# Routed attention: GpSimd's inverse roots move ahead of the low part of the keys

## The chip, the cores and the metric

The kernel runs on one core of a Trainium2 chip. The metric is the time of one execution on the device in microseconds (us). Five engines work side by side, each on its own list of instructions in a fixed order: TensorE (PE in the rows; PEld is its weight load), VectorE (DVE), ScalarE (ACT), GpSimd (POOL) and SyncE (SP, which here only issues transfers). They meet at semaphores. An engine that waits for one holds up everything behind it in its own list.

## The reference, cut to what matters

The program is a stack of four layers, each an attention and a feed-forward part, on x of 8 batches x 256 tokens x 256 features. The change lies in the third layer's second part, an attention whose output is scaled by a gate (a "routed" attention). For each of the 8 batches:

```
q, k, v = heads(x @ Wq.T + bq), heads(x @ Wk.T + bk), heads(x @ Wv.T + bv)   # 16 heads of 16
q_norm  = q / norm(q, axis=-1)                                               # one root per token and head
q_scaled = (q_norm + query_embedding) * softplus(temperature)
attn = softmax(q_scaled @ k.T / sqrt(16));  h = attn @ v
out = h * masked_gates.sum(-1) ;  x = x + out @ Wp.T + bp
```

The root that the change is about is `1 / norm(q)`: 128 partitions x 2 tiles of tokens x 16 heads, so 128x32 numbers for each batch.

## The kernel before, in words

`attention16` works on two layers in one pipeline: a plain attention (batches 0 to 7) and the routed one (batches 8 to 15, called the first to eighth routed batch here). `head_steps` builds one list of steps. In step s, eight slots n = 0 to 7 are filled: the products of scores for head pair n of batch s - 3 (`score`), the products for the row maxima of head pair n of batch s - 2 (`max`), and behind them the slot's extras from the table `ROUTED_EXTRAS` (routed batches) or `HEAD_EXTRAS` (plain ones). An extra ("k", 0) is the keys of batch s, ("y", 5) the output product of batch s - 5. Every compute engine walks the same list from top to bottom and takes the items that concern it. So the table sets the order on every engine at once.

For the queries of a routed batch the items are, in this order:
- `q`: TensorE makes the queries, tokens on the partitions; VectorE adds the bias into `qtm` (L922).
- `square`: ScalarE squares them into `qsq` (L732).
- `sums`: VectorE sums the squares over each head into `qn` (L930).
- `roots`: GpSimd makes the inverse roots: a first guess (`root_guess`, L1449), three times the four instructions of `root` (L1467 to L1473), one product with the temperature (L685). That is 14 instructions on 128x32 numbers, one behind another.
- `scale`: VectorE multiplies `qtm` by the roots (L936). A TensorTensor with both inputs in SBUF.
- `qT`: TensorE turns `qtm` over (L337), ScalarE copies the result twice (`qf`, whole, and `qs`, rounded), GpSimd subtracts the two for the low part of the queries (L653, tile `a_sb_qs`).

For the keys, item `k`: TensorE (L788), ScalarE's two copies `kf` and `ks` (L717), and GpSimd's low part (L653, tile `a_sb_ks`, helper `rest`). When that is done, SP may send the keys out to device memory (`k_out`, L591), from where later issues bring them back in another order (`k_in`, L603 and L604). GpSimd has three more items: `norm` (the next batch's normalised rows, L220 to L230, roots, L209), `v` (adds the output bias to x, L692), and `qT` above.

SP has a list of its own, `MOVES`, that is the same for every step. For a routed step it reads: row of maxima out and in for the second half of the heads, keys in, queries out, queries in, then `neg0_out` (L609: the negated maxima of the first eight heads to device memory), `k_out`, `neg0_in` (L615: back into one row of `QP`). TensorE waits for `neg0_in` before item `score0` of the next step (L861), and before `max0` it waits until VectorE has read the product of the `max` item before (L838 and L1018; one PSUM tile `MX` serves all of them).

Slot 7 of a routed step holds `score7`, `max7`, `qT`, `factor`. In the first four routed steps the output product `y` of a plain batch (L795) follows there, before the next step's `score0`; in the last four `score0` follows at once.

Of the kernel before, what the change touches and what calls it, by code (L numbers as in the profile page):

```python
# [362 lines left out]
def at_least(eng, sem, count):  # L363
    if count > 0:
# [4 lines left out]
               2: [("weigh0", 3), ("T0", 4), ("T1", 4)], 3: [("k", 0)], 4: [("neg0", 2), ("weigh1", 3), ("aT", 4)],  # L369
               5: [("v", 0), ("out0", 3), ("norm", -1)], 6: [("weigh2", 3)], 7: [("y", 4)]}  # L370
ROUTED_EXTRAS = {0: [("neg1", 3), ("xT", 0), ("weigh3", 4), ("y", 5)], 1: [("q", 0), ("out1", 4), ("norm", -1)],
# [3 lines left out]
MOVES = [("ctx", -1, (False,)), ("neg1_out", 3, (False, True)), ("q_in", 1, (False,)), ("neg1_in", 3, (False, True)),  # L375
         ("k_in", 1, (False, True)), ("q_out", 1, (True,)), ("q_in", 1, (True,)), ("q_out", 0, (False,)),
# [2753 lines left out]
```

How the kernel before makes its waits and increments, by code:

```python
        @block.vector  # L166
        def _(dve):
            dve.wait_ge(loaded, 32)
            for t in range(NT):
                dve.bn_stats(g.stats[:, t, :], g.x[:, t, :])
# [2 lines left out]
def norm_factors(dve, g, sqrt_in, sqrt_out):  # L173
# [2 lines left out]
    dve.tensor_tensor(g.mean[:], st[:, :, 1], st[:, :, 4], ALU.add)  # L176
    dve.tensor_tensor(tmp[:, 0, :], st[:, :, 1], st[:, :, 4], ALU.subtract)
    dve.tensor_tensor(tmp[:, 1, :], st[:, :, 2], st[:, :, 5], ALU.add)
    dve.drain()
    dve.tensor_scalar(g.mean[:], g.mean[:], 0.5, None, ALU.mult)
    dve.tensor_tensor(tmp[:, 0, :], tmp[:, 0, :], tmp[:, 0, :], ALU.mult)
    dve.tensor_scalar(tmp[:, 1, :], tmp[:, 1, :], 1.0 / D, EPS, ALU.mult, ALU.add)
    dve.drain()
    dve.scalar_tensor_tensor(out=tmp[:, 1, :], in0=tmp[:, 0, :], scalar=0.25, in1=tmp[:, 1, :],
                             op0=ALU.mult, op1=ALU.add).then_inc(sqrt_in, 1)
    dve.wait_ge(sqrt_out, 1)
    dve.reciprocal(g.rstd[:], tmp[:, 2, :])
    dve.drain()
# [10 lines left out]
def norm_sqrt(act, g, sqrt_in, sqrt_out):  # L200
    act.wait_ge(sqrt_in, 1)
    act.activation(g.tmp[:, 2, :], g.tmp[:, 1, :], ACT.Sqrt).then_inc(sqrt_out, 1)
# [67 lines left out]
    def add(self, dve, g, b):  # L270
        dve.wait_ge(self.landed[b], 16 * TT * self.n)
        xb = g.x[:, b * TT:(b + 1) * TT, :]
        if self.layer == 1:
            dve.tensor_tensor(xb, xb, self.rows[:, b, 0], ALU.add)
# [88 lines left out]
def at_least(eng, sem, count):  # L363
    if count > 0:
        eng.wait_ge(sem, count)
# [164 lines left out]
        def scored(eng, b):  # L530
            eng.wait_ge(ex_full[1], 8 * (b + 1))
```

## Time and profile before

| | |
|---|---|
| median of 3 runs | 1793.23 us (1793.08 to 1796.47) |
| the profiled execution | 1801.62 us, of it 1799.9 in the span |
| PE busy | 1456.1 us (81%) |
| DVE | 979.6 us (54%) |
| ACT | 703.6 us (39%) |
| POOL | 551.8 us (31%) |
| mean granted TensorE clock | 0.893 of full speed |

The profile is of one execution; the span is the part that the trace covers. A busy share is over the whole span and does not tell which wait counts; the stretch of the routed batches is read by itself. The tile names in rows have no layer number: `a_sb_qn` there is the tile `a2_sb_qn` of this pipeline. The routed batches' roots run from 1043.9 to 1216.4 us.

### The profile page before, as it was taken

What the parts mean: (1) busy time and instruction counts of PE and PEld (TensorE: products, weight loads), DVE (VectorE), ACT (ScalarE), POOL (GpSimd) and SP (SyncE); (2) the same over time, 40 slices, a digit from 0 to 9 for tenths busy, and PEclk for the clock granted to TensorE, in tenths of its full rate; (3) what the DMA queues carried; (4) which work ended last, traced back from release to release, by engine and by line L of the source; (5) the groups of instructions that cost most, each with busy time, mean ns of one, the idle gap of its engine ahead of it and who ended that gap; (6) DMA issues with size and microseconds to landing.
All of it is one profiled execution on the core that took longest, in us unless ns stands there. A gap on an engine that the chain in (4) does not pass through costs nothing. (4 is left out here: it accounts for less than half of the span.)

```text
span 1799.9 us, 33526 instructions
## 1 busy us (share of the span) xinstructions
PE 1456.1 (81%) x12090; PEld 1131.0 (63%) x12090; DVE 979.6 (54%) x2007; ACT 703.6 (39%) x1554; POOL 551.8 (31%) x905
## 2 busy tenths in 40 slices
PE   3898676692889844997479999898769999999876
PEld 2565455581666524997346666665468888888765
DVE  2676463353765652221666676776346666666652
ACT  1465443230456520211246666664443333333111
POOL 2110016105655403000511455540035454444210
PEclk9799988796899966999689999997779999999976
DMA  5332093344865228994755555552030000000001
GB/s 142 87 73 50 2 365 130 115 133 150 189 147 134 60 87 310 339 351 168 212 121 131 122 105 119 120 117 51 2 114 7 8 8 7 8 1 2 2 7 47
DMA packets 89772, 195.49 MB, mean 109 GB/s; under 512 B 14000, under 2 KB 62513, under 8 KB 81041
## 3 DMA queue, kind: packets, MB, share of 16 engines
q1 hardware_dynamic: 76688, 172.97, 34.1%
q0 software_dynamic: 4608, 12.59, 2.2%
q10 hardware_dynamic: 8320, 7.87, 1.3%
q8 instruction: 96, 1.57, 0.4%
q14 instruction: 60, 0.48, 0.1%
HBM read 136.37 MB, written 57.02 MB: 107 GB/s over the span
## 5 line engine op out<-in xcount | busy, mean ns | idle before, releaser
L1018 DVE TENSOR_REDUCE a_sb_mx<-a_mx 128x4 f32<-128x1024 f32 x192 | 234.8, 1223 | 119.6 <-PE a_mx L838 117.1
L759 ACT ACTIVATE a_sb_probs<-a_ex 128x512 f32<-128x512 f32 x368 | 200.3, 599 | 150.8 <-PE a_ex L861 150.5
L1434 DVE RECIPROCAL a_sb_rden<-a_ot 128x256 f32<-128x256 f32 x64 | 111.5, 1742 | 60.8 <-PE a_ot L1297 60.8
L266 POOL DMA_INDIRECT a_sb_landing<-f_y_slots,g_pos x48 | 47.3, 985 | 264.0 <-POOLq L143 250.5
L838 PE MATMUL a_mx<-a_sb_KP,a_sb_QP 48*128 48x256 f32 x768 | 91.1, 315 | 36.4 <-DVE a_sb_mx L1018 24.3
L874 PE MATMUL a_ot<-a_sb_probs,a_sb_v 128*32 128x256 f32 x1536 | 112.9, 415 | 7.5 <-ACT a_sb_probs L759 7.5
L861 PE MATMUL a_ex<-a_sb_QP,a_sb_KP 49*128 49x256 f32 x736 | 95.7, 338 | 26.1 <-ACT a_sb_probs L759 20.3
L861 PEld LDWEIGHTS a_ex<-a_sb_QP,a_sb_KP 49*128 49x128 f32 x736 | 59.3, 194 | 78.2 <-issue 54.0
L1219 ACT ACTIVATE a_sb_whole<-a_gp 128x512 f32<-128x512 f32 x64 | 38.2, 598 | 170.4 <-PE a_gp L1241 170.4
L838 PEld LDWEIGHTS a_mx<-a_sb_KP,a_sb_QP 48*128 48x128 f32 x768 | 64.3, 201 | 48.8 <-DVE a_sb_mx L1018 25.9
L1173 POOL TENSOR_TENSOR a_sb_q_lo<-a_sb_whole,a_sb_q_hi 128x512 fp32r<-128x512 f32 x32 | 42.1, 1316 | 126.9 <-ACT a_sb_q_hi L1220 126.0
L1419 DVE TENSOR_REDUCE a_sb_mx<-a_sc 128x2 f32<-128x256 f32 (+1 forms) x128 | 62.0, 548 | 31.1 <-PE a_sc L1266 30.9
L1619 POOL TENSOR_SCALAR_AFFINE_SELECT a_sb_sim<-a_sb_sim 128x256 f32<-128x256 f32 x128 | 55.6, 464 | 63.9 <-ACT a_sb_sim L1674 63.9
L1231 ACT ACTIVATE a_sb_probs<-a_sc 128x512 f32<-128x512 f32 x64 | 38.2, 598 | 94.3 <-PE a_sc L1281 62.3
L2812 PEld LDWEIGHTS f_hb<-f_sb_xsT,f_sb_wb 128*128 128x128 f32 x640 | 74.3, 195 | 0.8 <-issue 0.3
L2812 PE MATMUL f_hb<-f_sb_xsT,f_sb_wb 128*128 128x128 f32 x640 | 74.5, 278 | 0.0
L653 POOL TENSOR_TENSOR a_sb_qs<-a_sb_qf,a_sb_qs 128x512 fp32r<-128x512 f32 x24 | 30.7, 1279 | 137.9 <-ACT a_sb_qs L717 101.7
L874 PEld LDWEIGHTS a_ot<-a_sb_probs,a_sb_v 128*32 128x32 f32 x1536 | 42.5, 114 | 45.3 <-issue 14.1
L2825 PE MATMUL f_yb<-f_sb_wb,f_sb_hT 128*128 128x256 f32 x320 | 70.7, 379 | 0.0
L1181 POOL TENSOR_SCALAR_AFFINE_SELECT a_sb_probs<-a_sb_probs 128x256 f32<-128x256 f32 x128 | 48.8, 404 | 60.8 <-ACT a_sb_probs L1232 60.7
L2758 ACT ACTIVATE f_sb_hT<-f_hb,f_sb_wb 128x128 f32<-128x128 f32 x80 | 22.8, 368 | 112.1 <-PE f_hb L2812 112.1
L1303 PE MATMUL a_gp<-a_sb_wo,a_sb_oT 128*128 128x256 f32 x256 | 61.6, 396 | 5.5 <-issue 5.5
(445 smaller groups left out, 3655.5 us busy)
## 6 DMA issues: line engine op xcount, KB each, us to landing
f_sb_wb<-f_w SPq DMA_DIRECT2D x20, 2052.0 KB, 10.1
a_q_moved<-a_sb_qs SPq DMA_DIRECT2D x24, 512.0 KB, 5.9
a_sb_QP<-a_q_moved SPq DMA_DIRECT2D x48, 256.0 KB, 4.4
a_k_moved<-a_sb_ks SPq DMA_DIRECT2D x16, 512.0 KB, 5.1
a_sb_KP<-a_k_moved SPq DMA_DIRECT2D x32, 256.0 KB, 6.0
a_sb_kvT<-ctxT SPq DMA_DIRECT2D x24, 256.0 KB, 3.0
a_sb_QP<-a_q_moved SPq DMA_DIRECT2D x48, 128.0 KB, 5.1
f_x_slots<-f_sb_zero SPq DMA_DIRECT2D x1, 6144.0 KB, 20.6
```

The lines of the kernel that those rows point to most:

```text
L759: act.activation(probs[:, group % 3, 2 * (u % 2) + par], ex_of(par, b, u)[:], ACT.Exp, scale=scale)\
L838: op = pe.matmul(MX[:, par, t, :], QP[at:at + R, b % 3, u, t * P:(t + 1) * P], KP[at:at + R, b % KB, u % KM, :], start=True, stop=True)
L861: op = pe.matmul(ex_of(par, b, u)[:, t, :], KP[at:at + R + 1, b % KB, u % KM, t * P:(t + 1) * P], QP[at:at + R + 1, b % 3, u, :], start=Tr ...
L874: op = pe.matmul(OT[c // 2][32 * j:32 * j + 32, c % 2, :], v4[:, b % 4, t, (4 * c + j) % VH, :], probs[:, (4 * b + c) % 3, j, t, :], start ...
L1018: dve.tensor_reduce(pair, MX[:], AX.X, ALU.max, negate=True).then_inc(mx_read, 1)
L1181: op = pool.affine_select(later, later, [[0, 2], [1, P]], ALU.is_ge, 0.0, base=0, channel_multiplier=-1)
L1303: op = pe.matmul(GP[gp.slot(("y", b))][:, t, :], oT[:, c, t * P:(t + 1) * P], wo[:, c, :], start=(c == 0), stop=(c == C - 1))
L1419: op = dve.tensor_reduce(mx[:, t, 2 * i:2 * i + 2], SC[pair][:, :, t, 0:(t + 1) * P], AX.X, ALU.max, negate=True)
L1434: dve.reciprocal(rden[:, n], OT[n][:, 1, :])
L1619: op = pool.affine_select(later, later, [[0, 2], [1, P]], ALU.is_ge, 0.0, base=0, channel_multiplier=-1)
L2812: op = pe.matmul(HB[j % 2][c // (FC // 2)][:, c % (FC // 2), :], w1(j, k, c), xsT[:, j, k, :], start=(k == 0), stop=(k == KD - 1))
L2825: op = pe.matmul(YB[j % 2][:, 0], hT[:, j, c, :], w2(j, c), start=(c == 0), stop=(c == FC - 1))
```

## The change

In `ROUTED_EXTRAS`, `sums` and `roots` come first in slot 3 and `k` behind them. Before, `k` and `sums` stood in slot 3 and `roots` in slot 4.

```diff
@@ -369,8 +369,8 @@
- 2: [("square", 0), ("weigh0", 3), ("T0", 4), ("T1", 4)], 3: [("k", 0), ("sums", 0)],
- 4: [("neg0", 2), ("weigh1", 3), ("aT", 4), ("roots", 0)], 5: [("gate", 4), ("out0", 3)],
+ 2: [("square", 0), ("weigh0", 3), ("T0", 4), ("T1", 4)], 3: [("sums", 0), ("roots", 0), ("k", 0)],
+ 4: [("neg0", 2), ("weigh1", 3), ("aT", 4)], 5: [("gate", 4), ("out0", 3)],
```

On GpSimd, the place between two batches' low parts of the queries in the last four routed steps. Before (`a_sb_ks` is the low part of the keys, `a_sb_qn` the roots, `g_x_all` the bias on x):

```order
L653 TENSOR_TENSOR a_sb_ks<-a_sb_kf,a_sb_ks 128x512
L1449 TENSOR_SCALAR a_sb_qn<-a_sb_qn 128x32
L1467 TENSOR_TENSOR a_sb_qn<-a_sb_qn 128x32
...
L1473 TENSOR_TENSOR a_sb_qn<-a_sb_qn 128x32
L685 TENSOR_TENSOR a_sb_qn<-a_sb_qn,a_sb_spq 128x32
L692 TENSOR_TENSOR g_x_all<-g_x_all,a_sb_bo 128x512
L653 TENSOR_TENSOR a_sb_qs<-a_sb_qf,a_sb_qs 128x512
```

The same place on GpSimd after the change:

```order
L1449 TENSOR_SCALAR a_sb_qn<-a_sb_qn 128x32
L1467 TENSOR_TENSOR a_sb_qn<-a_sb_qn 128x32
...
L1473 TENSOR_TENSOR a_sb_qn<-a_sb_qn 128x32
L685 TENSOR_TENSOR a_sb_qn<-a_sb_qn,a_sb_spq 128x32
L653 TENSOR_TENSOR a_sb_ks<-a_sb_kf,a_sb_ks 128x512
L692 TENSOR_TENSOR g_x_all<-g_x_all,a_sb_bo 128x512
L653 TENSOR_TENSOR a_sb_qs<-a_sb_qf,a_sb_qs 128x512
```

The low part of the keys has moved from ahead of the 14 root instructions to behind them, and stands directly ahead of the bias on x. This is so in all eight routed batches; nothing else moves on GpSimd, and the lists of PE, DVE, ACT and SP are the same in both kernels.

On SP, the transfers around the keys' way out in a routed step, the same before and after (`a_neg_moved` are the negated maxima in device memory, `a_k_moved` the keys):

```order
L609 DMA a_neg_moved<-a_sb_negT 8x256
L591 DMA a_k_moved<-a_sb_ks 128x2x512
L615 DMA a_sb_QP<-a_neg_moved 1x1024 x2
L609 DMA a_neg_moved<-a_sb_negT 8x256
L615 DMA a_sb_QP<-a_neg_moved 1x1024 x2
L603 DMA a_sb_KP<-a_k_moved 32x2048
```

Nothing has moved in this list, but its second row waits for the instruction that has moved on GpSimd, and the third row stands behind it.

## Rows read from the trace of the kernel before

**Rows 1.** the tile of roots and sums (`a_sb_qn`), 900 to 1250 us: durations ns min/median/max; waiters

```profile
L936 DVE TENSOR_TENSOR a_sb_qtm<-a_sb_qtm,a_sb_qn x8: 693/1742/1748, 1049.2 to 1216.4; 128x512 f32<-128x512 f32 x8
...
  DVE a_sb_qtm L936: 13.2, 8
  PE a_gp L337: 7.2, 6
```

**Rows 2.** groups of PE, 1042 to 1221 us: busy, mean ns, idle before, releaser

```profile
L838 PE MATMUL a_mx<-a_sb_KP,a_sb_QP 48*128 48x256 f32 x240 | 26.1, 293 | 3.0 <-DVE a_sb_mx L1018 3.0
```

**Rows 3.** the timeline, fifth routed batch: start, length, engine, line; idle in brackets

```profile
1132.66 1.10 DVE L930 TENSOR_REDUCE a_sb_qn<-a_sb_qsq 128x32 f32<-128x512 f32 x1
1134.86 1.28 POOL L653 TENSOR_TENSOR a_sb_ks<-a_sb_kf,a_sb_ks 128x512 fp32r<-128x512 f32 x1 [1.82 <-ACT a_sb_ks L717]
1136.23 0.22 POOL L1449 TENSOR_SCALAR a_sb_qn<-a_sb_qn 128x32 int32<-128x32 int32 x1
...
1141.25 0.25 POOL L685 TENSOR_TENSOR a_sb_qn<-a_sb_qn,a_sb_spq 128x32 f32<-128x32 f32 x1
1141.45 1.27 POOL L692 TENSOR_TENSOR g_x_all<-g_x_all,a_sb_bo 128x512 f32<-128x512 f32 x1
1141.53 1.74 DVE L936 TENSOR_TENSOR a_sb_qtm<-a_sb_qtm,a_sb_qn 128x512 f32<-128x512 f32 x1 [1.53 <-POOL a_sb_qn L685]
1143.80 1.21 DVE L1018 TENSOR_REDUCE a_sb_mx<-a_mx 128x4 f32<-128x1024 f32 x1
...
1143.42 0.63 PE L337 MATMUL a_gp<-g_ident,a_sb_qtm 128*128 128x128 f32 x4 [1.35 <-DVE a_sb_qtm L936]
1143.98 0.50 PE L861 MATMUL a_ex<-a_sb_QP,a_sb_KP 49*128 49x256 f32 x4
1145.15 0.50 PE L838 MATMUL a_mx<-a_sb_KP,a_sb_QP 48*128 48x256 f32 x4 [0.67 <-DVE a_sb_mx L1018]
```

**Rows 4.** the timeline of PE, first and second routed batch

```profile
1051.08 0.63 PE L337 MATMUL a_gp<-g_ident,a_sb_qtm 128*128 128x128 f32 x4 [1.35 <-DVE a_sb_qtm L936]
...
1073.31 0.63 PE L337 MATMUL a_gp<-g_ident,a_sb_qtm 128*128 128x128 f32 x4 [0.30 <-DVE a_sb_qtm L936]
```

**Rows 5.** the timeline of DVE and POOL, where both want SBUF

```profile
1072.47 0.69 DVE L936 TENSOR_TENSOR a_sb_qtm<-a_sb_qtm,a_sb_qn 128x512 f32<-128x512 f32 x1 [1.77 <-POOL a_sb_qn L685]
1072.51 1.78 POOL L692 TENSOR_TENSOR g_x_all<-g_x_all,a_sb_bo 128x512 f32<-128x512 f32 x1
...
1145.73 1.28 POOL L653 TENSOR_TENSOR a_sb_qs<-a_sb_qf,a_sb_qs 128x512 fp32r<-128x512 f32 x1 [3.01 <-ACT a_sb_qs L717]
1145.80 1.24 DVE L966 SCALAR_TENSOR_TENSOR a_sb_sm<-a_sb_sm 128x2 f32<-128x2 f32 x1
1146.97 0.20 POOL L220 TENSOR_TENSOR a_sb_ln<-g_ln_stats 128x2 f32<-128x2 f32 x1
```

**Rows 6.** the timeline of SP's queue, fifth routed batch

```profile
1136.86 0.27 SPq L609 DMA_DIRECT2D a_neg_moved<-a_sb_negT  x1
1137.23 0.38 SPq L591 DMA_DIRECT2D a_k_moved<-a_sb_ks  x1
1141.60 0.52 SPq L615 DMA_DIRECT2D a_sb_QP<-a_neg_moved  x2
```

**Rows 7.** DMA issues at 936.7, 980.4 and 1068.8 us, one each: KB, us to landing

```profile
a_k_moved<-a_sb_ks SPq DMA_DIRECT2D x1, 512.0 KB, 2.7
...
a_k_moved<-a_sb_ks SPq DMA_DIRECT2D x1, 512.0 KB, 3.6
...
a_k_moved<-a_sb_ks SPq DMA_DIRECT2D x1, 512.0 KB, 5.4
```

**Rows 8.** the timeline of PE: the same matmuls for the values, third and fifth batch

```profile
1091.57 3.68 PE L795 MATMUL a_gp<-a_sb_wv,a_sb_xnT 128*128 128x256 f32 x8
...
1139.41 1.99 PE L795 MATMUL a_gp<-a_sb_wv,a_sb_xnT 128*128 128x256 f32 x8
```

**Rows 9.** busy time by stretch: PE, PEld, DVE, ACT, POOL, then PEclk, DMA share, GB/s

```profile
1092.00:1096.00 4.00, 4.00 (x24) 2.46 (x23) 2.23 (x2) 0.46 (x1) 2.91 (x8) 0.62 0.92 201
```

## The prediction, made before the changed kernel was run

> **What bounds the kernel now.** I read the waits of the routed stretch first, since the change touches only eight batches of it. The view of the roots' tile says that VectorE waited for GpSimd's last root instruction eight times, 13.2 us in all, and that TensorE waited for the product that VectorE makes with these roots (L936, "scale") six times, 7.2 us in all [rows 1]. The second number counts. In this stretch TensorE is the engine that all others follow, and the other thing it waits for there from VectorE is a `max` product that has not been read: 3.0 us [rows 2].
>
> Then the timeline of one late routed batch, the fifth [rows 3]. VectorE's sums end at 1132.66 + 1.10 = 1133.76. GpSimd has been free since 1134.86 - 1.82 = 1133.04, yet it starts no root: the low part of the keys stands ahead and waits for ScalarE until 1134.86, then takes 1.28. The roots run from 1136.23 to 1141.50, 5.27 us. VectorE was ready for them at 1141.53 - 1.53 = 1140.00. Its scale then takes 1.74, where the shortest of the eight took 0.693 [rows 1], because GpSimd's bias on x (L692) starts 0.08 us ahead of it. TensorE was ready to turn the queries at 1143.42 - 1.35 = 1142.07. VectorE's late start goes on into its read of `max7` (1143.80, over at 1145.01), for which `max0` waits until 1145.15.
>
> **The change part by part.** No instruction is added or removed; the low part of the keys changes places with 14 root instructions.
>
> 1. The roots start when the sums end, at about 1133.85 (0.09 us from one instruction to the next, as from 1136.14 to 1136.23), and end at 1139.12 instead of 1141.50: 2.38 us earlier. That is before VectorE is ready (1140.00), so its wait of 1.53 goes.
>
> 2. The low part of the keys now runs from 1139.2 to 1140.5, so the scale at 1140.00 meets it. How long two such instructions hold each other up is in [rows 5]: where the scale started 0.04 us first, it took 0.69 and the bias on x 1.78, 0.51 more than its 1.27 [rows 3]; where GpSimd's low part (1145.73 to 1147.01) was first, a VectorE instruction on two numbers a partition took 1.24 and ended at 1147.04. So the scale ends at about 1140.5 + 0.69 = 1141.2, against 1143.27. Should the bias on x, which comes directly behind, get in first, it ends at 1142.5. I take 1141.2: the instruction at 1145.80 that waited was done within 0.03 us, although GpSimd's next one started at 1146.97.
>
> The Trainium skill (SBUF — State Buffer, section Who interferes with whom) says that of a VectorE instruction with two SBUF inputs and a GpSimd instruction that reads SBUF the one issued first keeps the other out completely, for its whole length. The rows above agree in both directions. By that rule the waiting scale goes ahead of the bias on x; were it the other way, the sum would be the third case below.
>
> 3. TensorE turns the queries at 1142.07: 1.35 earlier. The values' product is ready at 1139.41 + 1.99 = 1141.40 [rows 8], so VectorE's copy of it is over by 1142.1, `max7` is read from 1142.2 to 1143.4, and `max0` could start at 1143.55 instead of 1145.15: 1.6 earlier.
>
> 4. The price. The keys' low part ends at 1140.5 instead of 1136.14. SP sent the keys out at 1137.23 [rows 6]; now it can at about 1140.55, and `neg0_in`, issued at 1141.60 before, stands behind it. Of what TensorE needs soon this is the only transfer that moves; keys come back in only in the next step. `neg0_in` is two rows of 4 KB, but it now goes off directly behind 512 KB. The keys' way out takes 2.7 or 3.6 us to land where no large transfer is ahead of it, 5.4 in a routed step, where the queries' way in is [rows 7]. By 1140.55 those have had 3.7 us since `neg0_out`, which was issued behind them, so I count with 2.7 to 3.6: `neg0_in` lands at 1143.25 to 1144.15. TensorE wants it for `score0` at 1142.07 + 0.56 = 1142.63 (0.56 is from 1143.42 to 1143.98 [rows 3]), and `max0` can go 0.34 later (0.40 is the length of such a product, and PE's rows overlap). So `max0` starts at 1143.6 to 1144.5, middle 1144.0: 1.15 us earlier than 1145.15, with 1.6 and 0.65 as the ends. The end below nothing is the second case below.
>
> The Trainium skill (DMA: Bandwidth & Descriptors, section Queues, rings and completion order) states that a transfer's count lands only after every earlier write of the same DMA engine. That speaks against the change. It is why I let `neg0_in` land with the keys; without this rule the ends of the sum would be nearer to 1.6, nothing else in it would change.
>
> 5. The other batches. The sixth to eighth have the pattern of the fifth: the 7.2 us less 1.35 and 0.30 for the first two [rows 4] leave 5.55 over four, 1.39 each. In the first four steps an output product of 1.99 us, of a plain batch, follows the turned queries, so `neg0_in` has that much more room and the gain is what TensorE waits now: 1.35 and 0.30 [rows 4], and nothing in the third and fourth. There TensorE ran at its lower level: the values' product took 3.68 instead of 1.99 us [rows 8], in a stretch with a granted clock of 0.62, partly 1.2 GHz [rows 9], and VectorE caught up meanwhile.
>
> Sum: 1.35 + 0.30 + 4 x 1.15 = 6.25 us less; with the ends 4 x 0.65 + 1.65 = 4.25 and 4 x 1.6 + 1.65 = 8.05. It is made against the profiled execution: 1801.62 us, of which the span is 1799.9. That execution is 8.4 us above the median of 1793.23. The stretch is on the path in both, so I take the same 6.2 off the median: 1787.0 us, and a profile near 1795.4 if it is as much above its median.
>
> **The rivals.**
>
> - *`neg0_in` lands late: slower.* If 512 KB of keys take 5.4 us to land also when they go out last, `neg0_in` lands at 1145.95 and `max0` starts at 1146.3, 1.15 later than now. Four batches give 4.6 us; in the first four I count nothing gained, as the room is used up. 1793.2 + 4.6 = 1797.8. For it: the large transfers of a routed step share the queue, and 5.4 is a routed step's row. Against it: both rows with nothing ahead. It decides from 1145.15 - 0.34 - 1140.55 = 4.3 us to land: from there on the four late batches lose.
> - *The clock takes it or adds to it: no change.* One stretch at the lower level costs 3.68 - 1.99 = 1.7 us on one product [rows 8]. Every batch now starts at another moment, and TensorE has less idle time in front of it. Two such stretches more leave 6.2 - 3.4 = 2.8 us of gain, 1790.4, and with three it is 1792.1: not told from no change. Two fewer: 1783.6. The three runs before differ by 3.4 us, which is two of them. Nothing in the trace says which way it goes.
> - *The bias on x gets in ahead of the scale.* Then the scale ends at 1142.5, `max7` is read until 1144.3 and `max0` starts at 1144.45: 0.7 a batch, and about 1.0 instead of 1.35 in the first. 4 x 0.7 + 1.3 = 4.1 us less, 1789.1.
> - *The change does not do what it says.* If GpSimd were still at work when the sums end, the roots could not start. It is free 0.72 us ahead of them in the fifth batch [rows 3], so only a shift of that size would do it. Then nothing changes: 1793.
>
> **How the numbers follow.** From no change this kernel can be told at about 0.2%, 3.6 us. Forecast with its ends 0.55; `neg0_in` late 0.12; clock against it 0.15, clock for it 0.06; bias first 0.09; no effect 0.03. Faster by over 0.2% (below 1789.6): all of the forecast but its low end, the clock for it, and more than half of bias first: 0.66. Within 0.2%: the clock against it, no effect and the rest: 0.23. Slower by over 0.2%: most of the first rival: 0.11. The range goes from 1782 (the high end of the sum with two stretches fewer) to 1796.5, well into the case of a late `neg0_in`. The forecast's own range is 1785.2 to 1789.0.
>
> **What would show it.** Right: VectorE's wait for L685 (13.2 us) nearly gone, and L337's wait (7.2 us) under 1; the roots' L1449 starting 0.1 us behind L930 in all eight batches; L936 of 1.2 us or so, ending 0.7 behind the low part of the keys; SP's L591 for the keys some 3.3 us later in the step, and L615 directly behind it; PE L861 showing a short wait for `a_neg_moved`, 0.6 to 1.5 us in the last four. Wrong: such waits above 3 us (the first rival), L936 ending 0.7 behind L692 (the third), the same gaps gone and yet the same span, with more stretches under a clock of 1.0 (the second).

## The result, and the profile after

The changed kernel takes 1784.41 us against 1791.63 us of the kernel before, measured side by side: a ratio of 0.9954, with an interval of 0.9938 to 0.9971. By the ratio that is 8.2 us less, with 5.2 and 11.1 as the ends; the two medians differ by 7.2. The forecast was 6.2 less. The profiled execution of the changed kernel took 1786.56 us, of which the span is 1784.8.

The two spans differ by 15.1 us, and most of that is not the change. The sums of the first routed batch, with which its stretch begins, end at 1041.37 us before and at 1030.37 after. These 11.0 us lie ahead of the first instruction that moved. In two other profiles of the changed kernel the same moment is at 1040.74 and 1043.18. So from here on I measure from the first sums' end to the eighth `max0`: 178.68 us before, 171.81 after, 6.9 less. What comes behind that is 2.8 us longer in this profile of the changed kernel (11.0 + 6.9 - 2.8 = 15.1); in the two others, 578.5 and 579.7 us, it is as long as before (579.9).

The tile of the roots, 900 to 1250 us, in the changed kernel (durations in ns, then idle time by releaser, then who waited):

```profile
L936 DVE TENSOR_TENSOR a_sb_qtm<-a_sb_qtm,a_sb_qn x8: 886/1024/1368, 1036.4 to 1198.2; 128x512 f32<-128x512 f32 x8
...
  DVE a_sb_qn L930: 25.7, 8
...
  POOL a_sb_qn L1449: 25.7, 8
```

Against [rows 1]: nobody waits for L685 any more (13.2 us), and TensorE not for L936 (7.2 us). Now GpSimd waits for VectorE's sums, eight times. The scale takes 1.74 nowhere; its longest is 1.37.

What TensorE waited for between 1030 and 1203 us in the changed kernel (us, times, longest):

```profile
PE a_ex L861 <- ACT a_sb_probs L759: 5.5, 12, 1.0
PE a_ex L861 <- DMA a_sb_QP<-a_neg_moved: 3.3, 3, 1.2
PE a_mx L838 <- DVE a_sb_mx L1018: 0.3, 1, 0.3
```

The second line is new, the price that was foreseen. Three late batches show it; in the sixth, TensorE was late by a stretch at the lower clock and had nothing to wait for. The third line was 3.0 us [rows 2].

The timeline of the fifth routed batch in the changed kernel, to set beside [rows 3]:

```profile
1119.54 1.10 DVE L930 TENSOR_REDUCE a_sb_qn<-a_sb_qsq 128x32 f32<-128x512 f32 x1
1120.73 0.22 POOL L1449 TENSOR_SCALAR a_sb_qn<-a_sb_qn 128x32 int32<-128x32 int32 x1 [0.75 <-DVE a_sb_qn L930]
1125.76 0.25 POOL L685 TENSOR_TENSOR a_sb_qn<-a_sb_qn,a_sb_spq 128x32 f32<-128x32 f32 x1
1125.97 1.27 POOL L653 TENSOR_TENSOR a_sb_ks<-a_sb_kf,a_sb_ks 128x512 fp32r<-128x512 f32 x1
1126.89 0.89 DVE L936 TENSOR_TENSOR a_sb_qtm<-a_sb_qtm,a_sb_qn 128x512 f32<-128x512 f32 x1
1127.19 1.73 POOL L692 TENSOR_TENSOR g_x_all<-g_x_all,a_sb_bo 128x512 f32<-128x512 f32 x1
...
1128.88 0.66 PE L337 MATMUL a_gp<-g_ident,a_sb_qtm 128*128 128x128 f32 x4
1130.66 0.50 PE L861 MATMUL a_ex<-a_sb_QP,a_sb_KP 49*128 49x256 f32 x4 [1.13 <-DMA a_sb_QP<-a_neg_moved]
1131.00 0.40 PE L838 MATMUL a_mx<-a_sb_KP,a_sb_QP 48*128 48x256 f32 x4
1131.33 0.38 PE L847 MATMUL a_gp<-g_ident,a_sb_mx 128*8 128x128 f32 x2
1131.55 0.60 PE L337 MATMUL a_gp<-g_ident,a_sb_xn 128*128 128x128 f32 x4
```

SP's queue in the same batch, to set beside [rows 6]:

```profile
1123.55 0.27 SPq L609 DMA_DIRECT2D a_neg_moved<-a_sb_negT  x1
1127.31 0.38 SPq L591 DMA_DIRECT2D a_k_moved<-a_sb_ks  x1
1128.00 0.99 SPq L615 DMA_DIRECT2D a_sb_QP<-a_neg_moved  x2
```

The keys' way out itself lands sooner than in the third row of [rows 7]; this is the median over the eight of the stretch, and the same view of the kernel before (1040 to 1222 us) has 5.3:

```profile
a_k_moved<-a_sb_ks SPq DMA_DIRECT2D x8, 512.0 KB, 2.8
```

A quantity that the prediction did not use is the pace of the stretch: when TensorE starts to turn the next batch's normalised rows (L337 on `a_sb_xn`, "next xn" below). From there to the next sums' end it takes 12.2 to 12.3 us from the sixth and seventh batch, 12.6 from the fifth, and 10.26 or 10.51 in the early ones, before and after alike, wherever the clock is at its full level. Several chains lead to that start. One is TensorE's own order: next xn comes 0.55 to 0.65 behind `max0`, which waits for VectorE or stands behind a `score0` that waits. The other is the PSUM bank of the turned queries, which ScalarE has read when its second copy (`qs`) ends; next xn comes 0.05 behind that at the earliest. Here is that place in the kernel before, seventh batch:

```profile
1192.35 1.09 ACT L759 ACTIVATE a_sb_probs<-a_ex 128x512 f32<-128x512 f32 x2 [0.89 <-PE a_ex L861]
1194.57 0.84 ACT L717 ACTIVATE a_sb_qf<-a_gp,a_sb_qe 128x256 f32<-128x256 f32 x2 [1.14 <-PE a_gp L337]
1195.30 0.84 ACT L717 ACTIVATE a_sb_qs<-a_gp,a_sb_qe 128x256 fp32r<-128x256 f32 x2
...
1195.64 0.50 PE L838 MATMUL a_mx<-a_sb_KP,a_sb_QP 48*128 48x256 f32 x4 [0.67 <-DVE a_sb_mx L1018]
...
1196.29 0.60 PE L337 MATMUL a_gp<-g_ident,a_sb_xn 128*128 128x128 f32 x4
```

`qs` ends at 1196.14, and L337 follows at 1196.29, 0.65 behind `max0`: here `max0` holds it, and the bank would have let it start 0.1 earlier. Whether the bank holds it can be read from the wait of L337's weight load for `qs`. It does not occur in the kernel before between 1028 and 1222 us, and once in the changed kernel (in the sixth batch, behind the low stretch):

```profile
PEld a_gp L337 <- ACT a_sb_qs L717: 0.4, 1, 0.4
```

### The profile page after: what moved, and what is told of

Read it like the earlier page. It is cut to its first block and busy times, and to the rows that moved or that the text cites. A ratio compares the mean times of both kernels' runs of the same rounds, so it can differ in the third digit from the quotient of the medians.

```text
span 1784.8 us, 33526 instructions
## 1 busy us (share of the span) xinstructions
PE 1450.8 (81%) x12090; PEld 1128.6 (63%) x12090; DVE 973.1 (55%) x2007; ACT 703.6 (39%) x1554; POOL 558.5 (31%) x905
## 5 line engine op out<-in xcount | busy, mean ns | idle before, releaser
L838 PEld LDWEIGHTS a_mx<-a_sb_KP,a_sb_QP 48*128 48x128 f32 x768 | 64.3, 201 | 45.6 <-DVE a_sb_mx L1018 25.6
```

Source lines behind the costliest of these rows:

```text
L838: op = pe.matmul(MX[:, par, t, :], QP[at:at + R, b % 3, u, t * P:(t + 1) * P], KP[at:at + R, b % KB, u % KM, :], start=True, stop=True)
```

## The experiments

Each kernel is read by four times of its seventh batch where no other is named, counted from the end of its sums (all us, from the timelines, at the full clock but for the keys sent twice), and by the step from the seventh sums' end to the eighth. The step behind the fifth batch is longer: 24.64 before, 23.51 after.

| kernel | turned queries | score0 | max0 | next xn | step 7 to 8 | ratio to before |
|---|---|---|---|---|---|---|
| before | 9.66 | 10.23 | 11.40 | 12.05 | 24.27 | 1 |
| after, fifth batch | 8.24 | 10.02 | 10.36 | 10.91 | | 0.9954 |
| after, seventh | 8.24 | 9.86 | 10.20 | 10.75 | 22.99 | as above |
| short roots | 8.23 | 9.33 | 9.74 | 10.70 | 23.00 | 0.9921 |
| maxima first | 8.24 | 9.33 | 9.75 | 10.70 | 23.00 | 0.9945 |
| late bias | 8.60 | 9.32 | 10.33 | 10.98 | 23.30 | 0.9965 |
| maxima first and late bias | 8.24 | 9.33 | 9.75 | 10.70 | 22.98 | 0.9939 |
| before, maxima first | 9.68 | 10.25 | 11.42 | 12.07 | 24.30 | 1.0000 |
| keys twice | 8.25 | 11.21 | 11.80 | 12.75 | 27.23 | 1.0012 |
| half copy, maxima first | 8.24 | 9.33 | 9.75 | 10.40 | 22.65 | 0.9916 |
| half copy | 8.24 | 9.88 | 10.22 | 10.77 | 22.99 | 0.9953 |
| early bank, maxima first | 8.23 | 9.33 | 9.75 | 10.40 | 22.64 | 0.9933 |
| early banks, maxima first, late bias | 8.19 | 9.29 | 9.70 | 10.36 | 22.60 | 0.9922 |

The intervals of the ratios are 0.002 to 0.003 to either side. They tell most of the changed kernels from before, but hardly one changed kernel from another; the trace, whose steps repeat to 0.03 us, does.

**The changed kernel again.**

> The changed kernel once more, on the chip of the next three. My theory (TensorE's waits for the scaled queries go, and a part comes back as waits for the maxima behind the keys' way out): the stretch from the end of the first routed batch's sums (L930) to the last routed batch's max0 (L838 after the turned queries) is 178.7 us in the kernel before and 171.8 in the changed one; it should be 171 to 172.5 again, L861 waiting for a_neg_moved 3 to 4 us in all. Ratio to before 0.994 to 0.998. If the gain were a matter of the clock's luck, this stretch would differ between two profiles of the same kernel by 3 us or more, and the waits would not repeat.

Measured 0.9948 (0.9922 to 0.9974), and in a second comparison, 0.9967 (0.9937 to 0.9998). Its stretch is 168.97 and 170.08 us in the two profiles, against 171.81 in the first, with one, two and three stretches of about 3.4 us at the lower clock. I had expected 171 to 172.5, so this missed, and the 2.8 us between two profiles of one kernel are close to the 3 that I had named as a sign of the clock's luck. The length of the whole stretch is therefore a poor measure; the steps without a low stretch agree in all three profiles (21.7 early, 22.99 to 23.03 for the seventh). TensorE waits for `neg0_in` 1.0 to 1.4 us in these too, 4.7 and 3.2 us in all. The longest, 1.43 in a fifth batch, made that step 23.80 instead of 23.51 and 23.38.

> The changed kernel again, on the same chip as the three others, to compare them with. Ratio to before 0.993 to 0.997; late steps 23.0; between one and three stretches of 3.4 us at the lower clock in the routed stretch.

**One Newton step.** The kernel before, with the order unchanged:

```diff
-                        for _ in range(3):
+                        for _ in range(1):
                             root(pool, qn[:, 3], qn[:, 0], qn[:, 3], qn[:, 1])
```

(for the queries' roots; they are then less exact.)

> The kernel before, in its own order, with one Newton step in the queries' inverse roots instead of three (6 instructions instead of 14; the roots come out less exact). The roots then end at about 1136.2 + 2.2 = 1138.4 in the fifth batch's times, ahead of VectorE's 1140.0, and the low part of the keys is not moved. My theory: the lateness of the roots is all there is to win, so here the whole of it shows and no price: L337 waits for L936 under 0.5 us in all, L936 takes 0.69, no wait for a_neg_moved but at most the 0.5 of before; stretch 178.7 - 8.0 = 170.7 us (170 to 171.5), about 1 us under the changed kernel. Rival (the order of the keys itself brought the gain, for instance a keys' way out that no longer shares the queue with the queries' way in): the stretch stays above 175 us.

Ratio 0.9921 (0.989 to 0.9953), stretch 169.80 with two low stretches, just under what I expected. In the sixth to eighth batch the turned queries stand at 8.23 or 8.24 as in the changed kernel, with no wait for `neg0_in` (in the third and fifth there is one of 0.61 and 0.66, over the 0.5 expected). VectorE's scale starts at 7.15 here and ends 0.7 later than in the changed kernel, and the turned queries are no later. So 8.24 is not set by when the roots are ready: beyond some point earlier roots buy nothing, since TensorE has other items ahead.

**Maxima ahead of the keys.** The changed kernel, with `neg0_in` issued before `k_out` in routed steps:

```diff
-         ("neg0_out", 2, (False, True)), ("k_out", 0, (False, True)), ("neg0_in", 2, (False, True))]
+         ("neg0_out", 2, (False, True)), ("k_out", 0, (False,)), ("neg0_in", 2, (False, True)), ("k_out", 0, (True,))]
```

> The changed kernel with one more edit: in the routed steps SP issues the maxima's way in (neg0_in) ahead of the keys' way out (k_out). My theory: TensorE's waits for a_neg_moved (3.3 us in three late batches) come from the 512 KB of keys ahead of 8 KB in the queue; ahead of them the maxima land about 1.3 us after their issue, the waits go, and the stretch falls from 171.8 to 168.5 us (168 to 170). Ratio to before about 0.9935. Rival (the maxima wait for their own way out, or the landing has a fixed length of 3 us): the waits stay at 2 to 4 us and the stretch at 171 to 172.5. Second rival (the keys then land too late for the next step): new waits of PE for a_k_moved or of SP ahead of L603.

Ratio 0.9945 (0.9912 to 0.9979), stretch 170.95 with three low stretches. The waits for `neg0_in` are gone, and the steps are hardly shorter. The seventh batch in this kernel:

```profile
1177.37 0.66 PE L337 MATMUL a_gp<-g_ident,a_sb_qtm 128*128 128x128 f32 x4
1178.46 0.50 PE L861 MATMUL a_ex<-a_sb_QP,a_sb_KP 49*128 49x256 f32 x4 [0.44 <-ACT a_sb_probs L759]
...
1178.92 0.86 ACT L717 ACTIVATE a_sb_qs<-a_gp,a_sb_qe 128x256 fp32r<-128x256 f32 x2
...
1179.83 0.31 PEld L337 LDWEIGHTS a_gp<-g_ident,a_sb_xn 128*128 128x128 f32 x3 [0.42 <-ACT a_sb_qs L717]
1179.83 0.44 PE L337 MATMUL a_gp<-g_ident,a_sb_xn 128*128 128x128 f32 x2
```

and TensorE's waits for the bank, 1028 to 1222 us, one in each late batch that has a next xn:

```profile
PEld a_gp L337 <- ACT a_sb_qs L717: 1.3, 3, 0.4
```

`score0` now waits for ScalarE's exponentials of `score7`, and the next xn starts 2.46 behind the turned queries, where ScalarE's `qs` ends at 2.41. Now the bank holds it. In the changed kernel it is 2.51 and 2.67 (seventh and fifth batch), always 0.89 behind a `score0` that waited: there the transfer holds it, and the bank would have come 0.05 to 0.2 earlier. With the two other profiles the wait costs the fifth step 0.16, 0.45 and 0.03 us, the sixth 0.15 (once without a low stretch) and the seventh 0 to 0.03. This was half against my expectation, which had the stretch shrink to 168 to 170. At the last `max0`, which ends the stretch, the wait does show in full: 10.41 against 9.75.

The control, the same edit in the kernel before:

> A control: the kernel before with the maxima's way in ahead of the keys' way out. There the keys' way out has left 4.4 us ahead of the maxima's way in, and TensorE shows no wait for it. Both theories: late steps 24.3 to 24.6 as before, no wait for a_neg_moved, ratio 1.000 (0.998 to 1.002). A ratio under 0.998 would say that the order of SP's list is worth something by itself.

Ratio 1.0000 (0.997 to 1.003), late steps as before, stretch 180.06. The order of SP's list is worth nothing by itself.

**Late bias.** The kernel before; GpSimd's bias on x (L692) moves behind the low part of the queries in the routed batches, and the roots stay where they were:

```diff
                         rest(what, b, qf, qs, q_out, q_split)
+                        if routed(b):
+                            bias_x(b)
...
-                        xb = g.x[:, b % B * TT:(b % B + 1) * TT, :]
-                        pool.tensor_tensor(xb, xb, ...
+                        if not routed(b):
+                            bias_x(b)
```

> The kernel before with only the bias on x (L692 there) moved on GpSimd, in routed batches, from directly behind the roots to behind the low part of the queries. The roots are as late as before. Rival that I want to size (the gain came from the scale no longer sharing SBUF with the bias on x, 1.74 us against 0.69): L936 takes 0.69 in all eight batches, L337 waits 0.3 us in six batches instead of 1.35 in five, and the stretch falls by 1.05 in five batches, 5.2 us, to 173.5. My theory says the same for this part and that the other 1.5 to 1.8 us a batch of VectorE's wait (13.2 us in all for L685) stays: VectorE's wait for L685 remains 12.5 to 13.5 us, and the stretch stays 1.5 us or more above the changed kernel's 171.8. If the stretch came to 172 or less, the lateness of the roots would count for nothing.

Ratio 0.9965 (0.994 to 0.999). The tile of the roots in this kernel (its L942 and L692 are L936 and L685 of the others):

```profile
L942 DVE TENSOR_TENSOR a_sb_qtm<-a_sb_qtm,a_sb_qn x8: 692/693/694, 1038.1 to 1198.7; 128x512 f32<-128x512 f32 x8
...
  DVE a_sb_qtm L942: 13.2, 8
  PE a_gp L337: 2.4, 7
```

VectorE's wait for the roots is as long as before, 13.2 us, and yet the late batches turn their queries 1.06 earlier (8.60 against 9.66). The changed kernel gets 1.42. So three quarters of what the change gains at this point can be had by the scale no longer meeting the bias on x alone, and the earlier roots add a quarter. By the seventh step it is 0.97 of 1.28. Moving the bias alone would have brought most of it.

The stretch of this kernel is 171.01 us, and I had written beforehand that 172 or less would make the lateness of the roots count for nothing. That test was badly chosen: this profile has one low stretch, the first one of the changed kernel three. By the steps without one the order is as expected: 23.30 against 22.99 late, 22.23 against 21.73 early.

Both edits on the changed kernel:

> The changed kernel with both further edits: the maxima's way in ahead of the keys' way out, and the bias on x behind the low part of the queries (routed batches). Theory 1 (what holds a late batch now is ScalarE: the exponentials of score7 and two copies of the turned queries, which end 2.4 us after TensorE starts to turn the queries; waits ahead of that are covered): L936 0.69 instead of 0.89, no wait for a_neg_moved, late steps from sums to sums still 22.8 to 23.0, ratio to before 0.994 to 0.996, same as the changed kernel. Theory 2 (VectorE's and the transfer's remaining waits are on the path): steps of 22.0 or less in the late four, ratio 0.991.

Ratio 0.9939 (0.991 to 0.9969), late steps 22.98 to 23.00: the first theory. In four batches the scale took 1.64 to 1.75 all the same: the late bias holds back GpSimd's `norm`, the roots then start 0.8 us behind the sums, and the scale meets the keys' low part from its first moment. The steps did not change by it.

**Keys twice.** The changed kernel, with another 512 KB ahead of the real way out:

```diff
             def rows_out(b, split, parts, moved, out, was_in, per):
+                if out is k_out and routed(b):
+                    sp.wait_ge(split, b + 1)
+                    sp.dma_start(k_spare[b % 2].rearrange("a p s -> p a s"),
+                                 parts[:].bitcast(F32).rearrange("p a k s -> p a (k s)")).then_inc(out[b % 2], 16)
```

> The changed kernel, with the keys of a routed batch sent out twice: an extra 512 KB to spare device memory directly ahead of the real way out, so that neg0_in stands behind 1 MB. Theory 1 (the price of the change, TensorE's wait of 1.0 to 1.4 us for neg0_in, is covered only up to ScalarE's copies, and that cover is used up): neg0_in lands 1.4 to 2.6 us later, TensorE waits for it 2.5 to 3.8 us in each late batch, late steps grow from 23.0 to 24.3-25.6, the gain of the late batches is gone: ratio to before 0.998 to 1.001. Theory 2 (these waits do not count at all, whatever their size): waits of that size, steps of 23.0, ratio 0.995. Theory 3 (small transfers do not wait for large ones ahead, so the wait has another cause): wait for a_neg_moved stays near 1.1, steps 23.0.

Ratio 1.0012 (0.9985 to 1.0039): the whole gain is gone. The waits are 2.3 to 2.5 us, at or just under the low end of what I expected, and the ratio is just over its high end. The steps, 27.2 to 27.7, are far above the 25.6 that I gave as the upper end. The clock explains it. TensorE in the sixth batch, then the stretches around it (busy PE, PEld, DVE, ACT, POOL, then PEclk, DMA share, GB/s):

```profile
1168.69 0.66 PE L337 MATMUL a_gp<-g_ident,a_sb_qtm 128*128 128x128 f32 x4
1171.71 0.80 PE L869 MATMUL a_ex<-a_sb_QP,a_sb_KP 49*128 49x256 f32 x4 [2.36 <-DMA a_sb_QP<-a_neg_moved]
...
1173.25 1.06 PE L337 MATMUL a_gp<-g_ident,a_sb_xn 128*128 128x128 f32 x4
```

```profile
1165.00:1169.30 4.30, 4.30 (x40) 2.81 (x36) 3.55 (x7) 3.42 (x16) 3.42 (x5) 1.00 0.31 118
1169.40:1170.60 1.20, 0.00 (x0) 0.00 (x0) 1.05 (x5) 1.20 (x5) 0.00 (x0) 1.00 1.01 379
1170.60:1171.70 1.10, 0.00 (x0) 0.00 (x0) 0.49 (x4) 0.49 (x2) 0.53 (x1) 0.68 0.17 60
1171.70:1177.50 5.80, 5.79 (x33) 3.66 (x34) 1.23 (x1) 1.92 (x4) 3.92 (x18) 0.50 0.14 28
```

The granted clock falls from 1.00 to 0.50 of full speed, from 2.4 to 1.2 GHz, while TensorE stands idle in the wait, and stays there for about 6 us of dense work. The next xn starts at 12.75 instead of 10.75, and from there to the next sums it takes 14.4 to 14.5 instead of 12.24: a step of 27.2 is 22.99 + 2.0 + 2.2. Of the 2.0, 1.35 is the later `score0` (11.21 against 9.86) and 0.65 slower products behind it (1.54 instead of 0.89 from `score0` to next xn). So a further 1.35 us of wait goes into the pace in full, which tells the first theory from the other two, and the clock adds 2.9. Without the clock the step would come to 11.21 + 0.89 + 12.24 = 24.3, an estimate: that of the kernel before. In the early batches TensorE waits 0.5 to 0.7 us for `neg0_in` here, the clock stays up, and the steps are 22.1 to 22.3 instead of 21.7.

**Half copy.** ScalarE makes only the first tile of the whole copy `qf`; the second is left out of the computation. Once with the maxima first, once on the changed kernel as it is:

```diff
-                        for c in range(KD):
+                        for c in range(1 if what == "qT" and dst is whole_ else KD):
```

> The changed kernel with the maxima's way in ahead of the keys' way out, and with half of ScalarE's whole copy of the turned queries left out (qf of the second tile; the result of that half is not the reference's). ScalarE's two copies end 0.4 us earlier. Theory 1 (with no wait for neg0_in, the transposes of the next xn are held by these copies): L337 of xn starts 2.1 to 2.2 us after the turned queries instead of 2.46, late steps 22.6 to 22.75 instead of 23.0; the rest of the 0.4 is lost to TensorE's own order. Theory 2 (the copies are not what holds it): steps 23.0.

> The changed kernel as it is, the maxima's way in behind the keys' way out, with half of ScalarE's whole copy of the turned queries left out (qf of the second tile; that half of the result is not the reference's). With the maxima's way in ahead, the same cut brought the late steps from 23.0 to 22.65. Theory 1 (the wait for neg0_in and ScalarE's copies run side by side and end within 0.2 us of each other): now the wait, 1.0 to 1.4 us, is what ends last, L337 of xn stays 2.45 to 2.6 us behind the turned queries and the late steps stay 22.9 to 23.0; ratio to before 0.993 to 0.996. Theory 2 (the wait for neg0_in never counts): late steps of 22.65, as with the maxima first.

Ratios 0.9916 (0.9891 to 0.9941) and 0.9953 (0.9924 to 0.9981). The same cut in two places of the seventh batch, first with the maxima first:

```profile
1185.20 0.66 PE L337 MATMUL a_gp<-g_ident,a_sb_qtm 128*128 128x128 f32 x4
...
1187.36 0.60 PE L337 MATMUL a_gp<-g_ident,a_sb_xn 128*128 128x128 f32 x4
```

and with the keys ahead, as in the changed kernel:

```profile
1192.51 0.66 PE L337 MATMUL a_gp<-g_ident,a_sb_qtm 128*128 128x128 f32 x4
1194.15 0.50 PE L862 MATMUL a_ex<-a_sb_QP,a_sb_KP 49*128 49x256 f32 x4 [0.98 <-DMA a_sb_QP<-a_neg_moved]
...
1195.04 0.60 PE L337 MATMUL a_gp<-g_ident,a_sb_xn 128*128 128x128 f32 x4
```

2.16 and 2.53 behind the turned queries, steps 22.65 and 22.99. Both expectations held to a few hundredths. With the keys ahead, 0.4 less of ScalarE's copies buys nothing, because the wait for `neg0_in` holds the next xn already, by 0.05 us; with the maxima first the bank holds it, and the same 0.4 buys 0.35, until `max0` takes over (0.65 ahead of next xn, as in the kernel before).

**Early bank.** The same relief with the result kept: ScalarE copies the bank once, releases it, and makes the rounded copy from the first copy in SBUF.

```diff
+                if what in rounded:
+                    for c in range(KD):
+                        op = act.activation(whole[:, c, :], gp_of(what, b)[:, c, :], ACT.Identity, bias=biases[:, c:c + 1])
+                    op.then_inc(gp_read[gp.slot((what, b))], 1)
+                    read(act, what, b)
+                    act.activation(hi[:, 0], whole[:], ACT.Copy).then_inc(rounded[what], 1)
+                    return
```

> The changed kernel with the maxima's way in ahead of the keys' way out, and ScalarE's rounded copy of the turned queries made from the whole copy in SBUF, in one instruction, instead of from PSUM in two. The PSUM bank is then free after the first copy. Theory 1 (ScalarE's reading of that bank holds the next xn): L337 of xn 2.1 to 2.2 us behind the turned queries, late steps 22.6 to 22.75, early steps 21.7 as before; corrected stretch 164.5 to 165.5 against 165.8; ratio 0.990 to 0.994. Theory 2 (it is ScalarE's whole list, not the bank): the list gets 0.2 shorter at most, late steps 22.85 to 23.0.

> As the run with the early bank, with the keys' rounded copy made the same way (all sixteen batches), and the bias on x behind the low part of the queries in the routed batches. Expected: late steps 22.6 to 22.75, the scale L936 0.7 to 1.2; of the keys' copy no further gain, since TensorE shows no wait there: ratio 0.990 to 0.994. If TensorE's banks were short elsewhere too (rival), steps in the plain batches ahead of 1030 us would be shorter as well, and the ratio under 0.988.

The seventh batch with the early bank; the next xn starts before ScalarE's second copy has ended:

```profile
1181.94 0.84 ACT L718 ACTIVATE a_sb_qf<-a_gp,a_sb_qe 128x256 f32<-128x256 f32 x2
1182.81 0.63 ACT L721 ACTIVATE a_sb_qs<-a_sb_qf 128x512 fp32r<-128x512 f32 x1
...
1183.27 0.60 PE L337 MATMUL a_gp<-g_ident,a_sb_xn 128*128 128x128 f32 x4
```

Ratios 0.9933 (0.9901 to 0.9966) and 0.9922 (0.9891 to 0.9952); late steps 22.64 and 22.60, and no sign of the rival: the first sums end at 1036.87 and 1041.06, within the spread of the other kernels. The scale in the last kernel did not take the 0.7 to 1.2 that I expected but up to 1.74, for the reason given for both edits. The medians, 1790.34 and 1787.56 us, stand beside 1793.42 of the changed kernel on the same chip. The corrected stretches (less half of the time at the lower clock) are 164.97 and 165.04; worked out in the same way, with 1.7 us for each low stretch, the kernel with the maxima first has 165.8 and the changed kernel 166.7 to 167.3. By the steps the early bank gains about 0.35 us in each of three late steps, 1.1 us in all; by the ratios it can't be told from the changed kernel.

## Why the prediction was right

**The roots and VectorE's wait (step 1): right.** L1449 starts 0.09 us behind L930 (1120.73 against 1119.54 + 1.10), and L685 ends 5.37 behind the sums, where the working had 5.36. The wait of 13.2 us is gone. The clause that the change might not do what it says fell with it.

**The scale (step 2): right, 0.3 us better.** It was put at 7.44 behind the sums' end; it ends at 1127.78, which is 7.14. The keys' low part ended 0.14 earlier than reckoned, and the scale 0.54 behind it instead of 0.69. It took 0.89 and went ahead of the bias on x, which paid (1.73 instead of 1.27). The rival in which the bias gets in first did not occur: all eight biases were the ones held up. GpSimd's group of them between 1030 and 1203 us, with its mean of 1728 ns:

```profile
L692 POOL TENSOR_TENSOR g_x_all<-g_x_all,a_sb_bo 128x512 f32<-128x512 f32 x8 | 13.8, 1728 | 0.0
```

By what the Trainium skill (SBUF — State Buffer, Who interferes with whom) states, the one that was first would keep the other out for its whole length. L936 and L692 read nearly that way in the changed kernel: in the fifth batch the bias on x ends 1.14 us behind the scale, where its own length is 1.27.

**The turned queries (step 3): right.** 8.24 behind the sums' end against 9.66: 1.42 earlier, with 1.35 forecast.

**The price (step 4): right in mechanism and size.** In the fifth batch the keys go out at 6.67 behind the sums' end instead of 3.47, 3.2 later (3.3 forecast), in the sixth to eighth 4.1 later. `neg0_in` stands directly behind, and `score0` starts 3.35, 3.20 and 3.23 us after L591 in the fifth, seventh and eighth batch, inside 2.7 to 3.6. `max0` gains 11.39 - 10.36 = 1.03, 11.40 - 10.20 = 1.20 and 11.54 - 10.41 = 1.13, with 1.15 forecast. In both kernels `max0` leads the next xn at a full clock, so the milestone served. But the working saw only this chain. ScalarE's copies, which it never named, end only 0.05 to 0.2 us before they would have held the next xn themselves in this profile of the changed kernel. Without the price `max0` would gain 1.65, as forecast with 1.6, and the next xn only 12.05 - 10.70 = 1.35. So the price is 0 to 0.45 us of pace a batch, mostly under 0.2, where the working had 0.45, and the high end of 4 x 1.6 could not have been reached. That the forecast came out unharmed by this is in part luck.

The run with the keys sent twice bears the row out further: 512 KB more ahead, and `score0` starts 4.12 to 4.18 us after the real way out and 4.60 to 4.66 after the extra one. The Trainium skill (DMA: Bandwidth & Descriptors, Queues, rings and completion order) has a transfer's count wait for the earlier writes of its DMA engine. The trace agrees in that TensorE got its 8 KB later with every 512 KB more ahead; it does not show the rule itself.

**The early batches (step 5): the sum was near by luck; the term for the third and fourth failed.** Forecast were 1.35, 0.30, 0 and 0. Measured between the sums' ends:

| step | before | after | after, two other profiles |
|---|---|---|---|
| 1 to 2 | 23.33 | 21.81 | 23.43 (low), 21.82 |
| 2 to 3 | 22.22 | 23.36 (low) | 21.73, 21.71 |
| 3 to 4 | 23.42 (low) | 23.36 (low) | 21.73, 23.37 (low) |
| 4 to 5 | 23.42 (low) | 21.74 | 21.73, 21.73 |

"Low" marks steps with a stretch of about 3.4 us at the lower clock. One of the changed kernel's, the third batch, with the stretch ahead of it:

```profile
1077.50:1080.40 2.90, 1.75 (x18) 1.41 (x18) 1.30 (x2) 2.68 (x7) 1.82 (x8) 1.00 0.72 167
1080.40:1083.90 3.50, 3.50 (x14) 2.16 (x17) 2.60 (x3) 0.68 (x2) 3.25 (x4) 0.54 0.71 175
```

A clean step gains 1.5 in the first batch, 0.5 in the second and 1.7 in the third and fourth; a low one gains nothing and in the second batch loses 1.1. The prediction put nothing for the third and fourth, because TensorE was slow there in the one trace it had. That is no property of these batches: the fourth gains 1.68 already in the first profile of the changed kernel. Before, a low stretch ahead of the long scale cost 0.1 (23.42 against 23.33), because TensorE would have waited for the scale anyway; after, it costs 1.6. In the sixth batch of the kernel before, where it fell behind the turned queries, it cost 1.6 too (25.84 against 24.27). With no low stretch at all the four early steps would take 87.0 us instead of 92.2, 5.2 less, an estimate from the clean steps of the table with 23.33 for the third and fourth before. Two low stretches took 3.1 of that in the first profile. The gain is thus as uncertain as the clock.

**The sum: near.** 6.25 forecast; 6.9 between the two stretches, 9.7 and 8.6 with the other two profiles of the changed kernel, 8.2 (5.2 to 11.1) by the ratio of all runs. The four late batches (steps 5 to 8 and on to the last `max0`) gave 4.75, 5.9 and 4.8 us with 4.6 forecast, the early ones 2.1, 3.8 and 3.8 with 1.65. The 5.9 has a low stretch of the kernel before in it, which that profile of the changed kernel lacks. So the term of the late batches held, the early one was too small, and what is above 6.25 comes mainly from early batches without a low stretch. The time of 1787.0 against 1784.41 carries also the change of the kernel before itself, from 1793.23 to 1791.63.

**The rivals.** A late `neg0_in` did not occur, and the keys' way out took a median of 2.8 us, not 5.4. The run with the keys sent twice shows that the case was real. The working put the point of no gain at 4.3 us after the keys set out; at 4.6 a late step would be as long as before but for the clock, so that point was about right. What it left out is that the clock fell in each of the four late waits of this size: the step was 27.23 against 24.27. (The loss that step 4 calls the second case is the first in its list.) The clock as a rival was right in kind: it moves single profiles by 3 us, in either direction.

## What to carry to other kernels

When a wait goes, name the milestone from which everything later has a constant distance, here the next batch's first transposes, and then every chain that leads to it: the engine's own order, a transfer, a bank that another engine still reads. The gain ends where the next chain takes over. Two chains that end within 0.05 us of each other hide each other: taking away the transfer's wait alone, or shortening the copies alone, changed the seventh step by 0.01 us or less, both together by 0.34. Compare steps at the same clock, not whole stretches: one low stretch weighed more here than the gain of a batch. Look for the partner of a doubled duration first: the instruction that took 1.74 instead of 0.69 us gave three quarters of this gain, with the roots left where they were.

## What the runs showed of the hardware

- A wait of TensorE of 2.3 to 2.5 us behind dense work brought the granted clock from 1.00 to 0.50 in each of the four late batches of the run with the keys sent twice; waits of 1.0 to 1.4 us did not do so in the three profiles of the changed kernel.
- The same kernel had one, two or three low stretches of about 3.4 us in this part in three executions, in different batches. One cost 0.1 us where TensorE would have waited for VectorE anyway (23.42 against 23.33) and 1.6 elsewhere (23.37 against 21.73). What sets their places is not shown.
- Another 512 KB ahead in the same queue made the small transfer behind it 1.2 to 1.35 us later (waits of 2.3 to 2.5 instead of 1.0 to 1.2 us).
- A VectorE product of two SBUF tiles (128x512) that waited while GpSimd worked on a tile of that size went ahead of GpSimd's next one in all eight batches of the changed kernel; that one took 1.71 to 1.75 us instead of 1.27, the product 0.89 to 1.37 instead of 0.69.
